# Feed-forward gate split between ScalarE and GpSimd in a fused local-attention and GEGLU kernel

## What is computed

```python
def ffn_layer(x, g, bln, W1, b1, W2, b2):
    mu = x.mean(-1, keepdims=True)
    var = ((x - mu) ** 2).mean(-1, keepdims=True)
    xn = (x - mu) / jnp.sqrt(var + 1e-05) * g + bln
    hg = xn @ W1 + b1
    a, gate = jnp.split(hg, 2, -1)
    return a * jax.nn.gelu(gate, approximate=False) @ W2 + b2
for i in range(DEPTH):                                   # DEPTH = 6
    x = attn_layer(shift_tokens(x), Wqkv[i], q_scale[i], k_scale[i], Wo[i]) + x
    x = ffn_layer(shift_tokens(x), ln_g[i], ln_b[i], W1[i], b1[i], W2[i], b2[i]) + x
```

## Time and profile before

| | us |
|---|---|
| median of 3 runs | 4503.34 |
| profiled execution | 4507.01 |
| its span, first to last instruction | 4505.2 |

### The profile page before, as it was taken

One profiled execution on the slowest core, in us unless ns is written; L12 is line 12 of the kernel. 1 busy time (PEld: TensorE's weight loads), 2 busy tenths in 40 slices (PEclk: granted clock), 3 DMA queues, 4 the chain that ended last, 5 costly groups with the idle time before them and its releaser, 6 DMA issues. The chain is left out here.

```text
span 4505.2 us, 98224 instructions
## 1 busy us (share of the span) xinstructions
PE 4176.7 (93%) x35048; PEld 2719.6 (60%) x35048; DVE 4086.5 (91%) x5503; ACT 2795.8 (62%) x4035; POOL 2811.6 (62%) x4591
## 2 busy tenths in 40 slices
PE   5999999999979999999999999999999999999997
PEld 3555555555456666666666666666666666666664
DVE  5888788888779999999999999999999999999995
ACT  4666666666545666656666666666666666666663
POOL 3555555555556666666666666666666666676663
PEclk9999999999989999999999999999999999999998
DMA  1000000000010000100011000100001000001000
GB/s 54 3 6 5 3 3 5 5 3 3 14 39 15 16 16 20 36 19 16 15 30 28 16 17 15 32 27 16 17 19 38 17 15 17 19 18 37 16 16 14
DMA packets 173509, 81.44 MB, mean 18 GB/s; under 512 B 109120, under 2 KB 168512, under 8 KB 172224
## 3 DMA queue, kind: packets, MB, share of 16 engines
q1 hardware_dynamic: 173248, 78.08, 6.3%
HBM read 48.56 MB, written 16.91 MB: 15 GB/s over the span
## 5 line engine op out<-in xcount | busy, mean ns | idle before, releaser
L572 POOL TENSOR_TENSOR pn<-es,rden 128x1024 f32<-128x1024 f32 x192 | 366.7, 1910 | 691.7 <-DVE rden L903 691.7
L666 ACT ACTIVATE y<-ps 128x1024 f32<-128x1024 f32 x384 | 372.3, 1021 | 506.0 <-PE ps L1109 506.0
L556 POOL TENSOR_TENSOR t<-t,ardn 128x1024 f32<-128x1024 f32 x256 | 485.1, 1895 | 305.1 <-DVE ardn L788 304.8
L657 ACT ACTIVATE t<-ps,anm,srn 128x512 f32<-128x512 f32 x512 | 392.9, 771 | 272.3 <-DVE anm L797 272.3
L576 POOL TENSOR_TENSOR t<-t 128x1024 f32<-128x1024 f32 x192 | 454.8, 2369 | 87.8 <-DVE t L855 87.8
L855 DVE TENSOR_TENSOR t<-ps,tabl 128x512 f32<-128x512 f32 x768 | 491.0, 681 | 0.0
L853 DVE TENSOR_TENSOR t<-ps,tabl 128x1024 f32<-128x1024 f32 x384 | 467.1, 1216 | 15.9 <-ACT sq L682 13.0
L578 POOL TENSOR_TENSOR t<-t 128x1024 f32<-128x1024 f32 x192 | 453.1, 2360 | 2.1 <-DVE t L855 2.1
L957 DVE TENSOR_TENSOR qn<-t,rn 128x2048 f32<-128x2048 f32 x192 | 438.1, 2282 | 4.9 <-POOL rn L388 4.9
L913 DVE TENSOR_REDUCE ss<-sq 128x32 f32<-128x2048 f32 x192 | 437.0, 2276 | 0.0
L986 PEld LDWEIGHTS ps<-cst,qn 128*128 128x128 f32 x3072 | 350.0, 141 | 114.4 <-issue 58.6
(11 more groups left out here) (136 smaller groups left out, 8863.0 us busy)
## 6 DMA issues: line engine op xcount, KB each, us to landing
tokens_dram<-x SPq DMA_DIRECT2D x96, 128.0 KB
xs<-tokens_dram SPq DMA_DIRECT2D x192, 64.0 KB, 1.8
xw<-tokens_dram SPq DMA_DIRECT2D x192, 64.0 KB, 1.9
xsh<-x SPq DMA_DIRECT2D x48, 128.0 KB
xsh<-x SPq DMA_DIRECT2D x48, 127.0 KB
wm<-in_l_wqk SPq DMA_DIRECT2D x3, 1024.0 KB, 5.0
wv<-in_l_wv SPq DMA_DIRECT2D x6, 512.0 KB, 3.8
wo<-in_l_wo SPq DMA_DIRECT2D x6, 512.0 KB, 4.6
```

The lines of the kernel that those rows point to most:

```text
L556: nc.gpsimd.tensor_tensor(eA[:, v], eA[:, v], ardn[:, v].unsqueeze(2).to_broadcast([P, 2, SEQ]), ALU.mult).then_inc(a_pn, 1)
L657: e = act.activation(eA[:, j, h], bank(j % 2 * 2 + h), ACT.Exp, bias=anm[:, j, h:h + 1], scale=srn[:, a % 2, j, h:h + 1], accum_out=aden[: ...
```

## The change

The gate moves off VectorE. ScalarE follows each Gelu with an Identity activation that copies bank 6 with its bias `b1s` into `fh`, and raises a new semaphore `f_v`. GpSimd multiplies `fh` by `fg` in place and raises `f_h`; this product stands behind the Newton steps of `rn` in GpSimd's turn, and in c=0 ahead of the feed-forward's own Newton steps. TensorE's waits on the banks (`ffn_transpose`, `ffn_up`, and those ahead of the projections) look at `f_v` in place of `f_h`; `ffn_down` still waits for `f_h`. The wait that protects `fh` from being overwritten before `ffn_down` has read it (`f_o`) moves from VectorE to ScalarE.

```diff
@@ GpSimd
+            def gate(n, c):
+                pool.wait_ge(f_g, n * NC + (c + 1))
+                pool.wait_ge(f_v, n * NC + (c + 1))
+                nc.gpsimd.tensor_tensor(fh[0:CH[c], c], fh[0:CH[c], c], fg[0:CH[c], :], ALU.mult).then_inc(f_h, 1)
...
                     newton(pool, l_rs, t + 3, rn[:], ss[:], rt[:])
+                if c == 0 and s.ffn(2):
+                    gate(s.f2, 2)
+                if c >= 2 and s.ffn(1):
+                    gate(s.f1, c - 2)
                 if c == 0 and s.ffn(1):
                     n = s.f1
@@ ScalarE, gelu
                 act.activation(fg[0:CH[c], :], bank(7)[0:CH[c], :], ACT.Gelu,
                                bias=b1s[0:CH[c], NC + c:NC + c + 1]).then_inc(f_g, 1)
+                if c == 0:
+                    past(act, f_o, n)
+                act.activation(fh[0:CH[c], c], bank(6)[0:CH[c], :], ACT.Identity,
+                               bias=b1s[0:CH[c], c:c + 1]).then_inc(f_v, 1)
@@ VectorE
-            def gate(n, c):
-                dve.wait_ge(f_g, n * NC + (c + 1))
-                if c == 0:
-                    past(dve, f_o, n)
-                nc.vector.scalar_tensor_tensor(out=fh[0:CH[c], c], in0=bank(6)[0:CH[c], :], scalar=b1s[0:CH[c], c:c + 1],
-                                               in1=fg[0:CH[c], :], op0=ALU.add, op1=ALU.mult).then_inc(f_h, 1)
...
-                if c == 0 and s.ffn(2):
-                    gate(s.f2, 2)
...
-                if c >= 2 and s.ffn(1):
-                    gate(s.f1, c - 2)
@@ TensorE: ffn_transpose, ffn_up, and ahead of the projections
-                past(pe, f_h, n * NC)
+                past(pe, f_v, n * NC)
...
-                past(pe, f_h, n * NC + c)
+                past(pe, f_v, n * NC + c)
...
-                        pe.wait_ge(f_h, (s.f2 + 1) * NC)
+                        pe.wait_ge(f_v, (s.f2 + 1) * NC)
...
-                        pe.wait_ge(f_h, s.f1 * NC + (c - 1))
+                        pe.wait_ge(f_v, s.f1 * NC + (c - 1))
```

More of the change, by code:

```diff
@@ L312, in build @@
         f_g = sem("f_g")
+        f_v = sem("f_v")
         f_h = sem("f_h")
```

## The result

The change makes the kernel slower: 4578.2 us (median of 4 runs, 4576.9 to 4579.9) against 4504.9, a ratio of 1.0165 with a 95% interval of 1.0152 to 1.0177. That is +73 us; the profiled execution took 4579.9 us (span 4578.1) against 4507.0.

A forecast was written before the change was run, and what follows sets the result against it. TensorE was taken as a bound equal to VectorE, with the gate hidden. Terms 57 + 25 + 5 - 3 + 1 = +85 us on 4507.0 gave 4592 profiled, 4588 as median, stated as 4590; range 4522 to 4615.

The forecast's parts named there:

- TensorE an equal bound, the gate hidden: In mid-layer turns TensorE takes the same 15.48 us as VectorE, so removing the gate gains only 0 to 0.2 us a turn.
- The product's price: GpSimd's multiplication of two full 128x512 operands: between 1.04 and 1.28 us, taken as 1.27 us.
- ScalarE hidden: The added Identity copy of 0.69 us leaves `xT` 0.65 us ahead of L1109, and the Exp table load hidden: no cost.
- `qn` blocked in c=2 and c=3: `qn` waits out GpSimd's product at the shared SBUF port: +0.73 us in each of 78 unfolded gated turns, +57 us.
- Who is first: In c=2 and c=3 GpSimd's product starts ahead of `qn`, by some 0.2 us.
- The first rival: `qn` goes first or neither blocks the other, so c=2 and c=3 cost nothing: +24 us, 4527 us; chance 0.14.
- c=0 and c=1: The product in c=0 delays GpSimd's queue by 1.2 us; the next turn c=1 loses 0.7 us, +25 us over 36 turns.
- nothing special: 36 of the 46 turns c=1 behind a gated c=0, taken as ordinary ones losing 0.7 us each.
- Turns (1, 1): 5 turns that pass the delay from c=0 on to `ffn_bias`, for which TensorE waits: +5 us.
- Turns (7, 1): 5 turns where the tables' products meet late Newton steps and L587 in place of L591 and `pn`: -3 us (-4 to +4).
- The end: Last chunks run alone, Identity where the gate stood, and the last product 0.5 us longer than the gate: +1 us.

The follow-up runs named there:

- experiment 3: Changed kernel with GpSimd's products of c=2 and c=3 held until `qn` ended and the gate of c=0 back on VectorE: 4502.2 us, ratio 1.0001.
- experiment 4: Kernel before the change with VectorE's gate cut from 512 to 16 columns, nothing added anywhere: 4502.4 us, ratio 1.0000.
- experiment 5: Kernel before plus ScalarE's Identity copy of bank 6 into a scratch tile; VectorE's gate and TensorE's bank reuse wait for it: 4510.4 us, ratio 1.0016.
- experiment 1: Changed kernel with GpSimd's product of c=2 and c=3 held until `qn` on VectorE has ended, c=0 as changed: 4535.2 us, ratio 1.0072.
- experiment 6: Changed kernel with GpSimd's product over 256 of the 512 columns, the gate left out of the other half: 4515.8 us, ratio 1.0031.
- experiment 7: Changed kernel with GpSimd's product of c=2 and c=3 replaced by a 4-column product and a 128x1536 memset: 4532.5 us, ratio 1.0064.
- experiment 8: Kernel before with VectorE's `scale_tables` moved from the head of turn (7, 1) to turn (7, 0) behind `pT`: 4494.5 us, ratio 0.9981.

## Why the prediction was right

The predicted time was 4590 us, the measured one 4578, within the range and in its sign. By its steps:

- **TensorE an equal bound, the gate hidden.** Right, and shown by experiments 3 and 4. The small gain of "0 to 0.2 us a turn" was 0: in both, the median of the unfolded gated turns c=2 and c=3 stayed at 15.48 to 15.49 us.
- **The product's price.** The line between the Newton step and L576 gave 1.28 us, I took 1.27, and it measured 1.272 (0.73 at 256 columns).
- **ScalarE hidden.** Right in the steady turns: `xT` still comes ahead of L1112, Identity needed no table load. Experiment 5 shows that the one place where it isn't hidden is the kernel's end.
- **`qn` blocked in c=2 and c=3.** The mechanism was right (experiments 1, 6, 7). The term was 78 x 0.73 = 57 us and measured 47.6, 0.61 a turn. The tail of 2.15 us behind the product was right. Mis-sized was the next step: `den` started at 2632.95, 0.07 us ahead of `qn`'s recorded end, while I compared with 3143.89 before, where it started at that end. The product also began 0.03 us earlier behind `den` than I had it.
- **Who is first.** I gave the product 0.2 us of lead. In c=2 it has 0.29 us (2629.60 against 2629.89). In most turns c=3 it has only 0.07 or 0.08; the timeline of a turn c=3 of the kernel after:

```profile
2645.48 0.25 POOL L389 TENSOR_TENSOR rn<-rn,rt 128x32 f32<-128x32 f32 x1
2645.70 1.27 POOL L571 TENSOR_TENSOR fh<-fh,qk 128x512 f32<-128x512 f32 x1
...
2645.77 3.35 DVE L960 TENSOR_TENSOR qn<-t,rn 128x2048 f32<-128x2048 f32 x1
```

  There VectorE comes out of the blocked `qn` earlier relative to TensorE, and `mx` has no wait for the scores; I had carried c=2's distances over to c=3. The margin is thin, but it is not luck alone: `qn` waits for the same last Newton step (2645.48 to 2645.73) that stands ahead of the product in GpSimd's queue, so VectorE can't come earlier than just behind that step's end, however early it is ready. It started 0.04 us behind it, and in all 78 turns the product was first, by 0.07 us at least. My text had VectorE's own lateness decide the order and left this wait out. The first rival (4527) needed the product's two waits to cost only some 0.1 us in c=3, not 0.2.
- **c=0 and c=1.** 25 us forecast, 26.1 measured; L915 over 2 us: 2.38. The mechanism was right and so were the 0.7 us of an ordinary turn (0.69). The total is in part luck: I counted 36 turns with "nothing special", and the five of the last layer cost 1.3 us each, while some others came out below 0.7.
- **Turns (1, 1).** 5 us forecast, 9.9 measured. The product's own delay is the 1 us a turn that I gave it: at full clock such a turn took 20.15 us before and 21.15 after. But these turns came out at 20.1 or at 21.8 us within the kernel before already (the one of the first layer at 21.1). In them TensorE waits for the bias; the stretch of the kernel after in which that wait falls, in two such turns (columns as above):

```profile
2473.10:2477.10 4.00, 4.00 (x56) 2.81 (x52) 1.29 (x2) 0.00 (x0) 0.00 (x0) 0.50 0.01 4
...
1931.40:1935.40 4.00, 4.00 (x29) 1.71 (x22) 3.63 (x3) 1.80 (x2) 0.00 (x0) 1.00 0.07 18
```

  The first belongs to a turn of 24.3 us and ran at half the clock, 1.2 GHz; the second to one of 21.2 us at 2.4 GHz. In both TensorE had waited just before, and the product makes that wait longer: in the 4 us ahead of such a stretch TensorE was busy for 3.2 to 3.4 us in the kernel before and for 2.0 to 2.3 us after. That this made the fall more likely is suggested and not shown. Which of these turns are slow differs from profile to profile; leaving out the first layer, 17 of 30 took 21.7 to 21.9 us in the six profiles without a product in c=0 (the others 20.1 to 20.3), and 13 of 15 took 21.4 to 24.3 us in the three with the full one (the others 21.2).
- **Turns (7, 1).** -3 forecast, -7.4 measured, outside my -4 to +4. The step that failed: I let the tables meet L587. In the groups of the kernel after, their products run nearly undisturbed at 0.64 and 0.42 us (1.48 on the mean before for the second):

```profile
L857 DVE TENSOR_TENSOR tabl<-tab,qks 128x256 f32<-128x256 f32 x12 | 4.5, 416 | 0.0
L853 DVE TENSOR_TENSOR tabl<-tab,qks 128x512 f32<-128x512 f32 x6 | 3.9, 643 | 0.0
```

  GpSimd is so late that the tables meet the short Newton steps of the feed-forward; a turn (7, 1) of the kernel after:

```profile
2324.05 0.64 DVE L853 TENSOR_TENSOR tabl<-tab,qks 128x512 f32<-128x512 f32 x1
...
2324.18 0.56 POOL L389 TENSOR_TENSOR frt<-c,frt 128x4 f32<-128x4 f32 x1
```

  Experiment 8 got about the same gain without the product.
- **The end.** +1 forecast, +3.1 measured. The last `ffn_down` waits 2.84 us for the product, where it had waited 1.65 us for the gate, and then takes 4.54 us in place of 2.9, at a granted clock of 0.77 in place of 0.86. I had priced the wait and not the clock.

Larger and smaller misses cancel in part: the sum was +85, the span grew by 72.9, of which 5.3 less lie in the untouched first stage.

## What to carry to other kernels

Work moved off an engine that is 91% busy is worth only what the second-highest engine leaves free in that turn; cut the work to nothing in a trial first, as in experiment 4, and see if the time moves. An instruction placed on GpSimd has to be checked against what VectorE runs at that moment: a VectorE instruction with two SBUF operands and a GpSimd one that reads SBUF run one after the other, so put the GpSimd work beside VectorE's reductions or PSUM readers (`den` kept its 1.22 us beside the product, L867 its 1.22 us beside `pn`), and small two-operand VectorE work beside short GpSimd steps. Small instructions with one SBUF operand have to be looked at too, as L922 shows. And where an engine's queue has no gap, an added instruction delays all that stands behind it, so its price can show up a turn later and on another engine.

## What the runs showed of the hardware

- The blocking depends on what GpSimd does, not on its being busy: beside a product `qn` took 3.13 and 3.35 us, beside a memset of 1.38 us 2.28. The Trainium skill (SBUF — State Buffer, Who interferes with whom) states just this, that a VectorE instruction with two SBUF inputs contends with a GpSimd one that reads SBUF and not with one that only writes it; both halves are now seen in this kernel.
- The blocking is not confined to two SBUF operands: L922, a TENSOR_SCALAR on 128x32 elements with one SBUF operand, took 2.38 us and ended with GpSimd's addition L584, against 0.25 undisturbed.
- `qn` ended 2.14 and 2.15 us behind products of 1.27 and 0.73 us, against 2.28 undisturbed, so about 0.14 us of it was already done when the product ended. The profile shows such a wait inside the instruction's own duration and not as idle time.
- A product of two full 128x512 operands took 1.27 us on GpSimd, one with a broadcast operand 1.04.
- With gaps between short bursts of matmuls at the end of the kernel TensorE's granted clock was 0.56 of full speed in experiment 5, where the kernel before had 1.00 and 0.86. The kernel before had 0.56 as well, in the 10 us from 4477, behind a wait of 12.4 us.
